# Second stage: VectorE sums the corners, table entries overlap, and all engines work on three batches at once

## The reference

```python
offset = conv2d(x, offset_w, offset_b)                  # 18 channels
mask = 2.0 * sigmoid(conv2d(x, mod_w, mod_b))           # 9 channels
py, px = offset + place of the tap + place of the pixel # 9 taps, 32x32 pixels
y0, x0 = floor(py), floor(px); wy, wx = py - y0, px - x0
for yy, xx, wt in corners:                              # the 4 neighbours
    val = val + gather(x, yy * W + xx) * (wt * valid)   # 64 channels each
val = val * mask
y = einsum('bckhw,ock->bohw', val, reg_w)               # 576 -> 64 channels
```

## Time and profile before

| | |
|---|---|
| median of 3 runs (lowest, highest) | 3651.82 us (3649.66, 3657.69) |
| the profiled execution | 3653.92 us, its span 3652.1 us |
| PE, DVE, ACT, POOL busy | 56%, 42%, 23%, 46% of the span |
| second stage, first gather to its last DVE work | 460.68 us to 2357.27 us |

### The profile page before, as it was taken

One profiled execution on the slowest core, in us unless ns is written; L12 is line 12 of the kernel. 1 busy time (PEld: TensorE's weight loads), 2 busy tenths in 40 slices (PEclk: granted clock), 3 DMA queues, 4 the chain that ended last, 5 costly groups with the idle time before them and its releaser, 6 DMA issues. The chain is left out here.

```text
span 3652.1 us, 36691 instructions
## 1 busy us (share of the span) xinstructions
PE 2039.0 (56%) x14480; PEld 1282.6 (35%) x14480; DVE 1541.7 (42%) x1349; ACT 852.6 (23%) x1117; POOL 1682.0 (46%) x1342
## 2 busy tenths in 40 slices
PE   3666323444544444444534444561788888888887
PEld 2544212222232222232322223351454544544545
DVE  3222420221122202220222112374788888878885
ACT  3111301021111112021111111252333233233241
POOL 0000075555655565555655575233454554554542
PEclk9877656666766666666766676786899899999899
DMA  7999442333323232323323232203111311212212
GB/s 322 431 432 431 155 114 83 89 89 89 92 84 91 85 96 85 92 84 91 91 83 92 84 97 84 100 17 105 55 61 55 103 60 66 95 57 67 96 52 78
DMA packets 169913, 423.39 MB, mean 116 GB/s; under 512 B 92648, under 2 KB 111232, under 8 KB 152704
## 3 DMA queue, kind: packets, MB, share of 16 engines
q1 hardware_dynamic: 114560, 271.53, 20.2%
q0 software_dynamic: 55296, 151.07, 13.8%
HBM read 396.91 MB, written 25.58 MB: 116 GB/s over the span
## 5 line engine op out<-in xcount | busy, mean ns | idle before, releaser
L436 POOL DMA_INDIRECT gath<-table,idx x1152 | 1089.1, 945 | 798.9 <-PE p_col L594 348.6
L594 PE MATMUL p_col<-ident,gath 128*128 128x128 f32 x2304 | 398.9, 338 | 667.2 <-issue 440.0
L594 PEld LDWEIGHTS p_col<-ident,gath 128*128 128x128 f32 x2304 | 342.8, 177 | 736.6 <-issue 632.4
L537 DVE TENSOR_TENSOR xt<-xt,p_y 128x512 f32 (+1 forms) x16 | 11.0, 688 | 1380.8 <-remote 1363.0
L483 ACT ACTIVATE cols<-p_col 128x384 f32<-128x384 f32 x384 | 186.0, 491 | 1162.1 <-remote 557.6
L582 PE MATMUL p_y<-cols,wreg 128*64 128x512 f32 x576 | 306.4, 692 | 141.2 <-issue 86.0
L535 DVE TENSOR_TENSOR gath<-gath,p_stat 128x2304 f32<-128x2304 f32 x128 | 317.5, 2549 | 64.4 <-DMA gath<-table,idx 62.6
L1192 PE MATMUL p_state<-xt,tri 128*128 128x512 f32 x512 | 257.4, 650 | 64.5 <-DVE prod L1080 64.5
L960 POOL TENSOR_TENSOR query<-query,expo 128x2048 f32<-128x2048 f32 x16 | 102.1, 6379 | 334.7 <-DVE query L1058 334.7
L1080 DVE TENSOR_TENSOR prod<-p_state,query 128x2048 f32<-128x2048 f32 x80 | 183.1, 2289 | 127.5 <-PE p_state L1197 127.5
L1228 PE MATMUL p_sum<-ident,prod 128*128 128x128 f32 x1024 | 171.0, 337 | 107.2 <-DVE prod L1102 107.2
(11 more groups left out here) (221 smaller groups left out, 2772.6 us busy)
## 6 DMA issues: line engine op xcount, KB each, us to landing
ring<-in_w SPq DMA_DIRECT2D x64, 2304.0 KB, 18.8
hidw<-in_hidw SPq DMA_DIRECT2D x64, 1024.0 KB, 4.8
gath<-table,idx POOLq DMA_INDIRECT x1152
table<-pix SPq DMA_DIRECT2D x256, 64.0 KB, 1.8
xt<-in_x SPq DMA_DIRECT2D x1, 4096.0 KB, 12.7
ring<-in_x SPq DMA_DIRECT2D x1, 4096.0 KB, 12.9
resid<-xt SPq DMA_DIRECT2D x32, 128.0 KB, 2.4
xlate<-resid SPq DMA_DIRECT2D x16, 256.0 KB, 2.9
```

The lines of the kernel that those rows point to most:

```text
L436: nc.gpsimd.indirect_dma_start(out=gath[:, t % SLOTS, k].rearrange("p n c -> p (n c)"), out_offset=None, in_=entries[u], in_offset=bass.In ...
L594: last = nc.tensor.matmul(p_col[g][:, k], corners, ident[:], start=(r == 0), stop=(r == 1), is_transpose=True)
```

## The change

- **Table.** An entry now holds two pixels, (y, x) and (y+1, x), 512 bytes, and a gather still takes 1 KB from the entry's start, so it also reads the entry of x+1 behind it. Each pixel is written twice, side by side. The pixels are transposed from a padded tile that holds row r in one half of the partitions and row r+1 in the other, so one transpose (4 of 128 x 128, twice a batch) gives both; the table is written with 5 DMAs a batch where it was 16.
- **Corner sum.** After the multiplication DVE sums the four corners of a tile with two TENSOR_REDUCEs: 8 taps (128 x 2048 numbers to 128 x 512) into `taps`, the ninth tap (128 x 256 to 128 x 64) into `taps8`. PE then transposes two taps at once: 4 transposes of 128 x 128 a tile and 4 a batch for the ninth tap, where it was 18 a tile. ACT copies once a tile and once for the ninth tap. The product with the weights takes 4 matmuls in the code for each half (with 128 rows) and 2 with 64 rows for the ninth tap, where it was 9 a half. Every transpose is a plain one; no sum is made on PE.
- **Slots.** POOL waits before tile t for `summed` of tile t of the batch before, which DVE raises.
- **Order.** `prep` is split. In batch b's main, ACT makes the padded tiles of b+1 ahead of tile 0, takes conv and pixels out before tile 2 and the sigmoid before tile 4. PE convolves b+1 first, then ends batch b-1 (second half, ninth tap), then transposes tiles 0 and 1, turns b+1's pixels and channels, and goes on with tile 2. DVE waits at the start of batch b for all 9 groups of `turned_taps` of b-1 (it writes `taps` anew), and between tiles 2 and 3 it adds the result of b-1 (`close`, waits for `y_done`) and computes the places of b+1 (`place`, waits for `off_turned`). The corner weights are made at the start of the batch (`weigh`), straight into PSUM.

The core of the diff (declarations of buffers and semaphores, and the host's layouts of the weights, are left out):

```diff
-        def over_batches(eng, prep, main):
-            prep(0, 0)
-            prep(1, 1)
-            main(0, 0)
+        def over_batches(eng, main):
+            main(0, 0, True)
             with eng.Fori(1, B // 2) as rr:
-                prep(rr * 2, 0)
-                main(rr * 2 - 1, 1)
-                prep(rr * 2 + 1, 1)
-                main(rr * 2, 0)
-            main(B - 1, 1)
+                main(rr * 2 - 1, 1, True)
+                main(rr * 2, 0, True)
+            main(B - 1, 1, False)
...
             def prep(b, u):
-                sp.wait_ge(pix_ready, b + 1)
+                sp.wait_ge(pix_ready, b * 2 + 2)
                 if not known(b):
                     sp.wait_ge(weighted, b * NT - NT)
-                for n in range(4):
-                    y0, x0 = 1 - n // 2, 1 - n % 2
-                    for r in range(4):
-                        dst = tables[u][y0:y0 + H, x0:x0 + W, n, :].rearrange("(t r) x c -> r x t c", r=4)[r]
-                        sp.dma_start(dst, pix[u][r * W:(r + 1) * W]).then_inc(table_out[u], 16)
-            over_batches(sp, prep, lambda b, u: None)
+                for r in range(4):
+                    dst = grid[u][1:1 + H, 1:1 + W].rearrange("(t r) x c -> r x t c", r=4)[r]
+                    sp.dma_start(dst, pix[u][r * W:(r + 1) * W]).then_inc(table_out[u], 16)
+                sp.dma_start(grid[u][0, 1:1 + W, C:2 * C], pix[u][0:W, 0, 0:C]).then_inc(table_out[u], 16)
+            def main(b, u, left):
+                if left:
+                    prep(b + 1, 1 - u)
+            prep(0, 0)
+            over_batches(sp, main)
...
-            def main(b, u):
+            pool.wait_ge(border_out, 160)
+            def main(b, u, left):
                 pool.wait_ge(coords_ready, b + 1)
                 if known(b):
-                    pool.wait_ge(table_out[u], 256 * (b // 2 + 1))
+                    pool.wait_ge(table_out[u], 16 * PIECES * (b // 2 + 1))
                 elif u == 0:
-                    pool.wait_ge(table_out[u], b * 128 + 256)
+                    pool.wait_ge(table_out[u], b * (8 * PIECES) + 16 * PIECES)
                 else:
-                    pool.wait_ge(table_out[u], (b + 1) * 128)
+                    pool.wait_ge(table_out[u], (b + 1) * (8 * PIECES))
                 for t in range(NT):
-                    if not (known(b) and b == 0 and t < SLOTS):
-                        pool.wait_ge(turned_taps, (b * NT + (t + 1 - SLOTS)) * 3)
+                    if not (known(b) and b == 0):
+                        pool.wait_ge(summed, b * NT + (t + 1 - SLOTS))
                         pool.sem_inc(slot_free, 1)
                     for k in range(TAPS):
                         nc.gpsimd.indirect_dma_start(
-                            out=gath[:, t % SLOTS, k].rearrange("p n c -> p (n c)"), out_offset=None, in_=entries[u],
+                            out=gath[:, t % SLOTS, k].rearrange("p n c -> p (n c)"), out_offset=None, in_=tables[u],
                             in_offset=bass.IndirectOffsetOnAxis(ap=idx[u][:, t, k:k + 1], axis=0),
                         ).then_inc(gath_in[t % SLOTS], 16)
...
+            def take(b, u):
                 act.wait_ge(conv_done, b + 1)
                 if not (known(b) and b == 0):
                     act.wait_ge(off_turned, b)
                 nc.scalar.activation(conv[:], p_conv[:], ACT.Copy).then_inc(conv_taken, 1)
+                for g in range(2):
+                    act.wait_ge(turned, b * 2 + (g + 1))
+                    if g == 0 and not known(b):
+                        act.wait_ge(table_out[u], b * (8 * PIECES) if u == 0 else (b - 1) * (8 * PIECES))
+                    nc.scalar.activation(pix[u][:, 4 * g:4 * g + 4], p_pix[:], ACT.Copy).then_inc(pix_ready, 1)
+            def open_gates(b):
                 act.wait_ge(off_ready, b + 1)
                 nc.scalar.activation(gate[:], off[:, :, 18:27], ACT.Sigmoid).then_inc(gate_ready, 1)
+            def main(b, u, left):
+                if left:
+                    pads(b + 1, 1 - u)
                 for t in range(NT):
                     h, q = t // 4, t % 4
+                    if t == 2 and left:
+                        take(b + 1, 1 - u)
+                    if t == 4 and left:
+                        open_gates(b + 1)
                     if q == 0 and not (known(b) and b == 0):
                         act.wait_ge(half_done, b * 2 + (h - 1))
+                    act.wait_ge(turned_taps, b * 9 + (t + 1))
+                    nc.scalar.activation(cols[h][:, :, q], p_col[t % 2][:], ACT.Copy).then_inc(cols_ready, 1)
+                if not (known(b) and b == 0):
+                    act.wait_ge(y_done, b)
+                act.wait_ge(turned_taps, b * 9 + 9)
+                nc.scalar.activation(cols8[:], p_col8[:], ACT.Copy).then_inc(cols_ready, 1)
+            pads(0, 0)
+            take(0, 0)
+            open_gates(0)
+            over_batches(act, main)
...
+            def place(b, u):
...
+                ts(idx[u][:], flat[:], float(WP + 1), None, ALU.add).then_inc(coords_ready, 1)
+            def weigh(b):
+                step = Chain(dve, own_dve, b * STEPS + (start + PLACE))
                 dve.wait_ge(gate_ready, b + 1)
                 step(ts(gate[:], gate[:], 2.0, None, ALU.mult))
                 step(tt(rowg[:, 0], rest[:, :, 0::2], gate[:], ALU.mult))
                 step(tt(rowg[:, 1], frac[:, :, 0::2], gate[:], ALU.mult))
                 for n in range(4):
+                    last = tt(p_wts.rearrange("p t (k n) -> p t k n", n=4)[:, :, :, n], rowg[:, n % 2],
+                              (frac if n // 2 else rest)[:, :, 1::2], ALU.mult)
+                last.then_inc(wts_ready, 1)
+                dve.wait_ge(wts_ready, b + 1)
+            def close(b):
+                mine = xt[:, bass.ds(b, 1), :].rearrange("p o x -> p (o x)")
+                dve.wait_ge(y_done, b + 1)
+                tt(mine, mine, p_y[:], ALU.add).then_inc(y_added, 1)
+                dve.wait_ge(y_added, b + 1)
+                nc.vector.bn_stats(row_stats[:, bass.ds(b, 1), :].rearrange("p o s -> p (o s)"), mine)
+            def main(b, u, left):
+                weigh(b)
+                if not (known(b) and b == 0):
+                    dve.wait_ge(turned_taps, b * 9)
                 for t in range(NT):
+                    if t == 3:
+                        if not (known(b) and b == 0):
+                            close(b - 1)
+                        if left:
+                            place(b + 1, 1 - u)
+                    dve.wait_ge(gath_in[t % SLOTS], b * (16 * TAPS) + 16 * TAPS)
                     g = gath[:, t % SLOTS].rearrange("p k n c -> p (k n) c")
                     w = p_wts[:, t].rearrange("p (m o) -> p m o", o=1).to_broadcast([P, 4 * TAPS, C])
+                    tt(g, g, w, ALU.mult).then_inc(weighted, 1)
+                    dve.wait_ge(weighted, b * NT + (t + 1))
+                    corners = gath[:, t % SLOTS].rearrange("p k n c -> p k c n")
+                    nc.vector.tensor_reduce(taps[:, t], corners[:, 0:2 * PAIRS], AX.X, ALU.add)
+                    nc.vector.tensor_reduce(taps8[:, t % 4, t // 4], corners[:, 2 * PAIRS], AX.X, ALU.add).then_inc(summed, 1)
+            place(0, 0)
+            over_batches(dve, main)
+            close(B - 1)
...
+            def turn(b, u):
+                def turn_pixels(g):
+                    if not (known(b) and b == 0 and g == 0):
+                        pe.wait_ge(pix_ready, b * 2 + g)
+                    for t in range(4 * g, 4 * g + 4):
+                        last = nc.tensor.transpose(p_pix[:, t % 4], rows2[u][:, 1 + 4 * t:5 + 4 * t].rearrange("p r w -> p (r w)"), ident[:])
+                    last.then_inc(turned, 1)
+                if not known(b):
+                    pe.wait_ge(off_ready, b - 1)
+                pe.wait_ge(conv_taken, b + 1)
+                turn_pixels(0)
+                for q in range(4):
+                    last = nc.tensor.transpose(p_off[:, u, q], conv[:, q * P:(q + 1) * P], ident[0:2 * LANE, 0:2 * LANE])
+                last.then_inc(off_turned, 1)
+                turn_pixels(1)
+            def half(b, h):
+                if h == 0 and not (known(b) and b == 0):
+                    pe.wait_ge(y_added, b)
+                pe.wait_ge(cols_ready, b * 9 + (9 if h else 4))
+                for k in range(PAIRS):
+                    last = nc.tensor.matmul(p_y[h * C:(h + 1) * C], wreg[:, k], cols[h][:, k].rearrange("p q x -> p (q x)"),
+                                            start=(k == 0), stop=False)
+                last.then_inc(half_done, 1)
+            def rest_of(b):
+                half(b, 1)
+                for h in range(2):
+                    part = slice(h * C, (h + 1) * C)
+                    last = nc.tensor.matmul(p_y[part], wreg[part, PAIRS], cols8[part].rearrange("p q x -> p (q x)"),
+                                            start=False, stop=True)
```

(84 more changed lines are left out.)

89 lines of the change are left out of this document (25 added, 64 removed).

## The result

| chip with the hold | before | after |
|---|---|---|
| median of 4 runs each (lowest, highest) | 3654.4 us (3649.7, 3657.7) | 3527.4 us (3526.9, 3528.9) |
| ratio, 95% interval | | 0.965 (0.964 to 0.967) |
| the profiled execution's span | 3652.1 us | 3527.0 us |
| first to last gather | 1851.6 us | 1749.1 us |
| end of the last gather to the stage's last DVE work | 45.0 us | 26.6 us |

The account below looks back on a forecast made before the run. Bound: POOL's gathers (90.0 us a batch) plus about 28 us of waits for PE. Savings of 100.6 to the last gather, 20 tail and 5 head make 126: 3653.9 to 3528, as median 3526 us; range 3340 to 3640.

Parts of the forecast that it names:

- the hold: While gathers run: a backlog of about 0.15 us per gather delays every PE completion, at its full 2.8 us a matmul.
- the drain: Behind POOL's last gather: PE completions wait 0.93 + 0.145 us per gather, 11.4 us for 72, 21.8 for 144.
- 88 matmuls a batch: PE's count after the change, where it was 216; 246 us a batch under the hold at its full 2.8 us.
- Its 36 of batch b: PE's 36 load-and-matmul pairs for batch b's tiles 2 to 7, half product and ninth tap: 30 to 40 us.
- DVE's sums: Two added TENSOR_REDUCEs a tile: 2.7 us, bounds 2.4 and 5.1; a tile 5.3 us, under POOL's 11.25.
- Stop and cycle: POOL stops 21.4 us after 72 gathers (11.4 drain, 10 hand-offs); a batch takes 111.5 us against 118.15 before.
- The tail: After the last gather: drain 11.4, last transposes, copy, 12 matmuls and close; 20 to 30 us, taken as 25, before 45.0.
- PE never in the way: Rival: completions flow with so few matmuls, the cycle is POOL's 90.0 us, 3208 us in all; chance 0.12.
- DVE's start waits for PE: Rival: DVE's tiles 0 to 2 fall behind POOL's stop, cycle 122.6 us, 3684 us in all; chance 0.09.
- Half a hold: Rival: plain transposes or 64-row matmuls held 1.4 us, stop 11 us, cycle 101, about 3381 us; chance 0.13.
- cut gathers: Rival: gathers split at the entry's 512 bytes, each up to 0.945 us longer, some 4300 us; chance 0.02.
- no net change: Case for the whole kernel: time moves by no more than 0.2%, 7 us; chance 0.03.

Follow-up runs that it names:

- e8: The kernel of e4 (PE sums the corners again, new order and table kept) on a chip with the hold: 3620.2 us against 3650.8 before, ratio 0.992.
- e7: Changed kernel plus 80 SP scratch writes a batch while gathers run, on a chip with the hold: 3560.5 us, where before takes 3644.
- e5: The changed kernel as it is, on a chip without the hold: 3211.9 us against 3216.4 for before, ratio 0.9987.
- e3: Changed kernel with each pair of taps transposed twice (120 matmuls a batch, not 88), on a chip without the hold: 3212.7 us, before 3215.2.
- e4: Changed kernel with PE summing the corners again (212 matmuls a batch), order and table kept, on a chip without the hold: 3211.8 us, before 3215.2.
- e6: Changed kernel with DVE's TENSOR_REDUCEs adding four neighbouring numbers, so without a stride: 3209.2 us where e5 took 3211.9.
- e9: Changed kernel with POOL clearing one scratch column and waiting for it after every third gather, on a chip without the hold: 3478 us.

## Why the prediction was right

- **The hold, and the rate at which it lets PE through.** Right for the chip it was read from: 2.8 us a matmul (11.2 us a group of 4), the drain 11.5 us for 11.4 forecast after 72 gathers, 22.4 for 21.8 after 144. What the prediction didn't see is that this depends on the chip and not on the kernel alone: of the five chips that came up in the experiments three don't have it. The forecast holds only where before takes some 3654 us, a condition that it doesn't name. The line of the drain is not a rule either: for a run of 45 it gives 7.5 us, and 6.0 were measured (e8).
- **88 matmuls a batch**: the window beside e7 counts 88. They are 26.7 us of work there and not the 13 that the prediction names, since it prices each as a transpose; its sum doesn't use that figure. Its 36 of batch b were done 41 us into the run (821.78), where 30 to 40 were forecast, partly because DVE was later.
- **DVE's sums** are the term that was mis-sized: 3.65 + 0.58 us a tile and not 2.7, a tile of 6.6 us and not 5.3, and the 2.3 us that it names as a sign did not come. It was between the bounds, and hidden as forecast: DVE sums tile 7 at 810, 30 us into the run, not 24, and waits behind it.
- **Stop and cycle**: 11.5 + 10.1 us for 11.4 + 10; cycle 111.3 for 111.5; first stop 32.5 for 31.8; 1749 us from first to last gather for 1751. The tail was 26.6 for 25, the head 4.2 for 5. Saved: 102.5 + 18.4 + 4.2 = 125.1 us of span, for 126. In the tail there is luck: its first part was forecast as the drain, 11.4 us, but what ended last was DVE, which still summed the batch's last tiles until 14.1 us after the last gather (2205.6 to 2219.7), a consequence of the mis-sized sums:

```profile
2219.10 0.58 DVE L572 TENSOR_REDUCE taps<-gath 128x64 f32<-128x256 f32 x1
2230.77 0.69 DVE L550 TENSOR_TENSOR xt<-xt,p_y 128x512 f32<-128x512 f32 x1 [11.09 <-PE p_y L627]
```

- **The rivals.** "PE never in the way" gave 3208 us, and that is what a chip without the hold shows (3211.9): its mechanism is right there, with before at 3215 as well. The rule of the Trainium skill that it went by ("SBUF — State Buffer", section "Who interferes with whom") agrees with chips 4, 8 and 15. With 6, 11 and the one of the result it doesn't: in the profile after, the four transposes L650 issued at 576.2 us are seen done at 608.2. Whether SBUF has a part in that no run shows. "DVE's start waits for PE" came nearer than the forecast said: DVE's first tile of the next batch waits 10.5 us at 821.89, but 48 us ahead of POOL's stop. "Half a hold", "cut gathers" (pitch 1.25 us) and no net change did not come.
- **Shown and open.** Shown: with the hold, DVE's sums and what goes with them bring about three quarters of the gain and order and table the rest (e8); without it both together bring 0.13% (e5) and the number of matmuls nothing (e3, e4); the hold goes by the matmul; landings and bytes of another queue are not what loads it (e7). Open: what in a gather holds PE's completions, why only on some chips, whether the recording has a part in it, and whether a wider pitch or a pause of POOL would end it; all six runs for that met chips without it.

## What to carry to other kernels

Before a wait is explained by a kernel, run the kernel unchanged on a second chip: here the same program takes 3651 or 3215 us, and a change that removes PE work under indirect DMAs is worth 3.5% or 0.13%. In the profiles here, long waits that end in `remote` and a row of gathers without its landing time mark the slower kind. A forecast summed from one trace (run, drain, hand-offs, tail, each from a row) can be right to 0.1% and still hold for that chip alone.

## What the runs showed of the hardware

- On chips 6 and 11, and on the one of the first result, PE's completions reach other engines late while POOL issues indirect DMAs: 2.8 us a matmul at its fullest, and a drain of 4.8, 11.5 and 22.4 us behind 27, 72 and 144 gathers. On chips 4, 8 and 15 not at all, on chip 4 with 212 matmuls a batch too (e4).
- A TENSOR_REDUCE of 2048 numbers to 512 at a stride of 64 numbers takes 3.63 us, unstrided 2.29 (e5 and e6, chip 8).
- A wait of POOL on its own MEMSET of one column (0.11 us) costs the next gather 0.6 us (1.85 against 1.25). In e9, with a longer POOL program, a gap of 3.9 to 4.1 us stands behind each 144 gathers, which is one turn of the loop, six in all; e5 has none. Two packets of the instruction queue q14 fall into each of them (here at 1201.7 and 1203.9 us), and this queue has 49 packets in e9 where it has 17 in e5. That POOL waits there for its program to be loaded is likely and not shown:

```profile
1200.24 0.11 POOL L447 MEMSET fill<- 128x1 f32 x1
1204.28 0.94 POOL L442 DMA_INDIRECT gath<-table,idx  x1 [3.92 <-issue]
```
